# One kernel, two reorderings: mask, weights and tiles loaded and multiplied chunk by chunk, and the small model's first turns split between the halves of the tiles beside them

## The reference

```
w  = w0 * repeat32x32(sum of each 32x32 block of mask > 0)
x1 = norm(x + x @ w.T)
x2 = norm(x1 + x1 @ w1.T + bias1 + adapter of the sequence)
x3 = norm(x2 + small_model(x2))
out = norm(x3 + x3 @ w3.T + bias3 + routed mixture of 8 adapters)
```

## Time and profile before

| | |
|---|---|
| median of 3 runs | 1832.55 us (1831.14 to 1834.01) |
| the profiled execution's own time | 1833.98 us |
| its span | 1832.3 us |
| PE busy | 1723.3 us, 94% of the span |
| DVE, ACT, POOL busy | 1066.5, 654.6, 436.3 us |
| granted PE clock, mean | 0.964 of full |
| share of the chain that ended last | PE 82%; issue, DVE, DMA 4% each |

### The profile page before, as it was taken

One profiled execution on the slowest core, in us unless ns is written; L12 is line 12 of the kernel. 1 busy time (PEld: TensorE's weight loads), 2 busy tenths in 40 slices (PEclk: granted clock), 3 DMA queues, 4 the chain that ended last, 5 costly groups with the idle time before them and its releaser, 6 DMA issues.

```text
span 1832.3 us, 23328 instructions
## 1 busy us (share of the span) xinstructions
PE 1723.3 (94%) x8154; PEld 1382.9 (75%) x8154; DVE 1066.5 (58%) x2049; ACT 654.6 (36%) x967; POOL 436.3 (24%) x380
## 2 busy tenths in 40 slices
PE   5999999999999999998699999997599899899898
PEld 4788888888888888887566666665478678678686
DVE  5433443345555555575577777766467567567553
ACT  2433333333333333222244545544233333333321
POOL 3111111100000000000366777743112112112110
PEclk9999999999999999999789999997699999899999
DMA  6323333333333332322010000004436536536421
GB/s 242 104 92 116 112 118 118 118 125 111 111 103 117 107 111 102 142 75 90 26 44 35 1 1 1 1 25 162 169 118 227 174 119 225 182 111 219 147 101 58
DMA packets 81543, 199.78 MB, mean 109 GB/s; under 512 B 9747, under 2 KB 26131, under 8 KB 81171
## 3 DMA queue, kind: packets, MB, share of 16 engines
q1 hardware_dynamic: 60690, 129.07, 21.5%
q10 hardware_dynamic: 20736, 69.22, 9.4%
HBM read 125.89 MB, written 72.35 MB: 108 GB/s over the span
## 4 chain that ended last, share of the span: by engine, by line
PE 82%; issue 4%; DVE 4%; DMA 4%; ACT 3%; POOL 2%; SPq 1%; ACTq 0%; POOLq 0%; DVEq 0%
PE ps L643 18%; PE ps L645 17%; PE ps L644 17%; PE ps L825 7%; PE ps L657 3%; PE ps L770 3%; PE ps L816 2%; PE ps L817 2%; PE ps L815 2%; DMA a_in<-in_expert_a 2%; PE ps L776 2%; PE ps L731 1%; PE ps L793 1%; PE ps L707 1%; PE ps L709 1%
## 5 line engine op out<-in xcount | busy, mean ns | idle before, releaser
L643 PE MATMUL ps<-wall_x,x_hi 128*128 128x512 f32 x1008 | 401.6, 398 | 10.7 <-DVE wall_x L1276 5.3
L645 PE MATMUL ps<-wall_x,x_lo 128*128 128x512 f32 x1008 | 396.1, 393 | 0.0
L644 PE MATMUL ps<-wall_x,x_hi 128*128 128x512 f32 x1008 | 395.7, 393 | 0.0
L1838 POOL TENSOR_TENSOR rstd<-var_eps,minus_half 128x1 f32<-128x1 f32 x96 | 77.2, 804 | 933.6 <-DVE minus_mean L1311 926.6
L1302 DVE BATCH_NORM_STATS2 stats<-row 128x6 f32<-128x512 f32 x192 | 133.0, 694 | 182.0 <-ACT row L996 177.6
L643 PEld LDWEIGHTS ps<-wall_x,x_hi 128*128 128x128 f32 x1008 | 191.5, 190 | 55.4 <-issue 13.3
L645 PEld LDWEIGHTS ps<-wall_x,x_lo 128*128 128x128 f32 x1008 | 191.2, 190 | 41.2
L644 PEld LDWEIGHTS ps<-wall_x,x_hi 128*128 128x128 f32 x1008 | 191.7, 190 | 38.4
L643 PE MATMUL ps<-wall_y,x_hi 128*128 128x512 f32 x512 | 204.0, 398 | 2.8 <-POOL wall_y L1845 2.8
L645 PE MATMUL ps<-wall_y,x_lo 128*128 128x512 f32 x512 | 200.4, 391 | 0.0
L644 PE MATMUL ps<-wall_y,x_hi 128*128 128x512 f32 x512 | 200.3, 391 | 0.0
(11 more groups left out here) (236 smaller groups left out, 2944.4 us busy)
## 6 DMA issues: line engine op xcount, KB each, us to landing
x_scratch<-row ACTq DMA_DIRECT2D x64, 512.0 KB, 2.8
x_in<-x_scratch SPq DMA_DIRECT2D x64, 512.0 KB, 4.0
w_in<-in_w_t SPq DMA_DIRECT2D x96, 256.0 KB, 3.0
cx<-x_scratch SPq DMA_DIRECT2D x32, 512.0 KB, 4.2
x_scratch<-cx ACTq DMA_DIRECT2D x32, 512.0 KB, 2.7
out<-row ACTq DMA_DIRECT2D x32, 512.0 KB, 2.6
x_in<-in_x_t SPq DMA_DIRECT2D x29, 512.0 KB, 3.4
w_more<-in_w_t SPq DMA_DIRECT2D x32, 256.0 KB, 3.6
```

Of the source, the lines that this page charges most:

```text
L643: pe.matmul(bank, hi[:, k], wall[:, k, 0, cols], start=(k == 0), stop=False)
L644: pe.matmul(bank, hi[:, k], wall[:, k, 1, cols], start=False, stop=False)
L645: return pe.matmul(bank, lo[:, k], wall[:, k, 0, cols], start=False, stop=(k == KC - 1))
L1838: pool.tensor_tensor(rstd[:, i:i + 1], var_eps[:, i:i + 1], minus_half[:, 0:1], ALU.pow)\
```

## The change

At the start, the loads go chunk by chunk with tile k beside chunk k, PE does two tiles of a chunk before the third, and DVE, ACT and PE have a new order. At the end of layer B, the early turns' steps are moved from the end of each tile's work to places between its halves, and the loads of `h` move from j = 4 to j = 5.

```diff
# SP
-            for k in range(2):
+            for k in range(KC):
                 load_w0(k)
-            for t in range(FIRST):
-                sp.dma_start(x_first[:, t], a["x_t"][t]).then_inc(first_loaded[t], 16)
-            for k in range(2, KC):
-                load_w0(k)
+                if k < FIRST:
+                    sp.dma_start(x_first[:, k], a["x_t"][k]).then_inc(first_loaded[k], 16)
...
-                if b + 1 == BATCHES and j == 4:
+                if b + 1 == BATCHES and j == 5:
                     sp.wait_ge(table_done, 1)
                     for n in range(UNITS - 2):
                         load_h(n)
# PE: first_products(k) becomes first_product(k, t), one tile
-            for k in range(3):
-                spread_blocks(k)
-            for k in range(KC):
-                first_products(k)
+            spread_blocks(0)
+            spread_blocks(1)
+            first_product(0, 0)
+            first_product(0, 1)
+            spread_blocks(2)
+            first_product(1, 0)
+            first_product(1, 1)
+            spread_blocks(3)
+            first_product(0, 2)
+            first_product(1, 2)
+            for k in range(2, KC):
+                first_product(k, 0)
+                if k + 2 < KC:
+                    spread_blocks(k + 2)
+                first_product(k, 1)
+                first_product(k, 2)
...
+                if s > B_END - EARLY:
+                    spread_rstd1(s - 1 - B_END + EARLY)
                 product(s, 1)
...
+                if s >= B_END - EARLY:
+                    variance1(s - B_END + EARLY)
                 if i >= 1:
                     turn_y(s - 1)
-                if s >= B_END - EARLY:
-                    turn_of(order, s - B_END + EARLY)
# ACT
-            w0_hi(0)
-            split_x(0)
-            w0_hi(1)
-            split_x(1)
-            split_x(2)
-            for k in range(2, KC):
+            for k in range(KC):
+                if k < FIRST:
+                    split_x(k)
                 w0_hi(k)
...
+                if s > B_END - EARLY:
+                    silu_x(s - 1 - B_END + EARLY)
+                if s >= B_END - EARLY:
+                    square1(s - B_END + EARLY)
                 if i >= 1:
                     split_y(s - 1)
-                if s >= B_END - EARLY:
-                    turn_of(order + order_end, s - B_END + EARLY)
# DVE: the loop over KC + 2 steps is replaced by
+            compare(0)
+            split_x(0)
+            add_identity(0)
+            block_sums(1)
+            w0_low(0)
+            compare(1)
+            split_x(1)
+            block_sums(2)
+            add_identity(1)
+            compare(2)
+            w0_low(1)
+            split_x(2)
+            block_sums(3)
+            add_identity(2)
+            compare(3)
+            for k in range(2, KC):
+                w0_low(k)
+                if k + 2 < KC:
+                    block_sums(k + 2)
                 if k + 1 < KC:
+                    add_identity(k + 1)
+                if k + 2 < KC:
+                    compare(k + 2)
...
                 half_stats(s, 0)
+                if s > B_END - EARLY:
+                    scale1(s - 1 - B_END + EARLY)
...
                 if s >= B_END - EARLY:
-                    turn_of(order + order_end, s - B_END + EARLY)
+                    turn = s - B_END + EARLY
+                    if turn == 2:
+                        scan(0)(0)
+                        scan(1)(0)
+                    if turn >= 1:
+                        rotate(turn - 1)
+                    take_var1(turn)
```

More of the change, by code:

```diff
@@ L624, in spread_blocks, with first_product @@
                   .then_inc(spread, 1)
-            def first_products(k):
+            def first_product(k, t):
                 pe.wait_ge(w0_hi_ready, k + 1)
                 pe.wait_ge(w0_lo_ready, k + 1)
[L629 to L638, removed]
+                if k == 0:
+                    pe.wait_ge(hi_ready, t + 1)
+                    pe.wait_ge(lo_ready, t + 1)
+                for half in range(2):
+                    last = terms(t, half, k, wall_x)
+                    if k == KC - 1:
+                        last.then_inc(mm_done, 1)
             def terms(s, half, k, wall):
@@ L1671, in _ @@
             block_sums(0)
-            for k in range(KC + 2):
-                if k + 1 < KC:
[L1674 to L1682, removed]
+            compare(0)
[17 more added lines that the diff above has]
+                    block_sums(k + 2)
+                if k + 1 < KC:
+                    add_identity(k + 1)
+                if k + 2 < KC:
+                    compare(k + 2)
             split_x(FIRST)
```

## The result

The changed kernel takes 1816.67 us (median of 7 runs, 1814.64 to 1820.36) against 1834.01 (7 runs of the kernel before beside it and earlier, 1824.74 to 1838.32). The ratio is 0.9911, 95% interval 0.9889 to 0.9933, which is 16.3 us gained (12.3 to 20.4); the two medians are 17.3 apart. The forecast was 1817.5, with 1812 to 1825 as range. The profiled execution's span is 1814.9 us (before 1832.3).

A forecast was written before the change was run, and what follows sets the result against it. PE was taken as the bound from 60 to 840 us and as starved at both ends of that stretch. Gains of 3.0 and 12.1 made 15.1, 1833.98 to 1818.9, or 1817.5 against the median 1832.55; range 1812 to 1825.

The forecast's parts named there:

- Sum: Whole kernel: 3.0 us from the start plus 12.1 from layer B's end, 15.1 gained; chance 0.68.
- The start until PE begins: Start: new load and engine order brings PE's first product at 12.4 us instead of 20.70, 8.3 earlier.
- The row's price for the hold: Start: DVE's low part, begun inside a POOL mask, took 1.75 us instead of 1.22, ending 1.07 after it.
- The start until its end: Start through chunk 7: done at 56.15 us instead of 58.98; 3.0 gained taken, bounds 1.5 and 5.1.
- Rival 1: Start gains nothing: DVE late at each chunk, PE stops and half rate lasts longer; 1820.5 us, chance 0.12.
- Nothing in it is tied to absolute time: PE's stretch from 60 to 840 us: moving its work earlier moves the end by as much.
- rival 4: Later stalls meet the clock's steps differently; slower by 0.2% needs 38 us more at half rate; chance 0.02.
- The end of layer B: Layer B's end: 10.7 us until turn_y(6) plus 1.4 behind it, 12.1 gained; bounds 9 to 14.
- The margins: Layer B's end: squares in time for variance1(0) by 0.5 us; rstd1(0) ready at 855.3, needed 856.3, margin 1.0.
- Rival 2: Layer B's end: stalls move, spread_rstd1 waits mid-tile between the halves; 1823 us, chance 0.11.
- rival 3: Turns 3 and 4: pipeline stands at DVE's mixes and PE's projection, part two worth 1; 1828.5 us, chance 0.05.
- the loads: Layer B's end: 4.7 us less from 848.21 to turn_x, plus 1.6 of half rate to 858.

The follow-up runs named there:

- Experiment 6: Changed kernel with POOL's masks of chunks 3 to 7 cut to one column in 32, the rest left unmasked; 1810.77 us in one run.
- experiment 1: Kernel before with only the start's part of the change, end of layer B as before; 0.9993, 1831.57 us.
- experiment 2: Kernel before with only the end of layer B changed (early turns' steps between the halves, loads of h at j = 5); 0.9931, 1820.62 us.
- experiment 4: Changed kernel with the loads of h put back to j = 4; 0.9948 of the kernel before, 1822.36 us.
- experiment 5: Changed kernel with DVE's mask sums behind compare from chunk 2 on and PE spreading three chunks ahead; 0.9894 of the kernel before, 1813.52 us.
- experiment 7: Changed kernel with DVE's mixes moved from the end of turn 3 to where DVE waited for the variance; 0.9902 of the kernel before, 1812.35 us.
- experiment 8: Changed kernel with the one-column bias product in two parts, half a product apart; 0.9926 of the kernel before, 1818.08 us.
- experiment 9: Changed kernel with both the mask sums behind compare and the mixes early; 0.9887 of the kernel before, 1810.91 us.
- experiment 10: On top of experiment 9, take_var1(2) ahead of tile 62's split and tile 63's statistics ahead of turn 2's recurrences; 0.9874 of the kernel before, 1808.80 us.
- experiment 3: Kernel before with one line changed, the loads of h at j = 5 instead of 4; 0.9991, 1832.11 us.
- experiment 11: Changed kernel again, unaltered, beside experiments 9 and 10; 0.9908 of the kernel before, 1814.49 us.

## Why the prediction was right

**Sum.** 15.1 was forecast, 16.3 measured (12.3 to 20.4). It is right for its main term, the end of layer B. That the whole came so close is in part luck: in the profile the kernel was 11.8 us ahead at the row of tile 63, not 15.1, because a half-rate stretch at 795 took 3.4, and gained 5.5 behind that row for which the sum has no term.

**The start until PE begins.** 12.4 forecast, 13.12 measured: the first mask and tile landed 0.2 and 1 us later than I had them, and the rest followed. The row's price for the hold was right in kind (both orders occur in the profile after).

**The start until its end.** 56.15 forecast, 56.15 measured, but by two errors that cancel. The clock rose before 17.5 (the spread at 17.46 takes 0.30), not at about 25, so chunk 2 began at 27.0, after 0.6 of waiting, and not at 28.3. And four periods were held, at 5.2, where I had counted three at 5.1 and one of 4.35. Experiment 6 shows the mechanism itself. Rival 1 (the start gains nothing) is wrong at its place.

**"Nothing in it is tied to absolute time."** This was the step that failed. In the changed kernel's two profiles and in experiments 1, 2 and 4 to 10 a half-rate stretch of 3.4 or 6.8 us follows the bias product near 795; in the kernel before and in experiment 3 it is missing. PE is busy there in all. So 2.8 us gained at 56 were 0.6 lost at 835 in the profile shown. All ten profiles with the new start have it and one of the three with the old one (experiment 2), so it does not need the new order, but that the new order makes it likelier is not excluded; what decides stays open.

**Behind the row of tile 63.** Here the sum has no term, and rival 4, which looked for a change of half rate there, priced only a loss. PE stands idle 72.5 us there before and 73.0 after, but is busy for 862.1 and 856.0, with 118.7 and 99.6 us at half rate: the clock makes the difference. It is not in the turns just behind the row, since the variance 90 us later comes within 0.2 us of the same place. Part of it is scatter, as the other profile of the changed kernel has 926.5 to go and 86.8 at half rate. But it is not one execution alone. Taking the gain by time (ratio) and subtracting the gain at the row of tile 63 in the one profile leaves 4.5 for the changed kernel, 5.0 for it in experiment 11, and 4.1, 4.4, 5.7 and 2.9 in experiments 2, 4, 5 and 8; in 1 and 3, where the steps were not moved, it leaves 1.2 and -2.1. So some 4 us seem to go with the moved steps, though each row is from one execution. By what way is not shown.

**The end of layer B.** 12.1 forecast, 12.4 measured from table to row, in the change and in experiment 2. The margins held: variance1(0) came at once, rstd1(0) was ready at 855.9, half a tile done at 856.9 (margin 1.0). The 6.49 us behind the last product stood as 6 to 7 in the forecast. Rival 2 (a wait between the halves) did not happen, rival 3 (given back in turns 3 and 4) not either: something like it happened to experiment 10. I had the loads at 4.7 + 1.6 = 6.3 as a term that stands by itself; alone they are worth 4.2 locally, and the rest needs the steps too. The term was right only within the whole.

**The Trainium skill.** SBUF — State Buffer, "Who interferes with whom", has the rule of the shared port that the first part rested on, and that a VectorE reduce never contends. This case agrees: a low part of 2.77 behind a mask, a mask of 2.88 behind a split, a mask sum of 1.20 beside a mask.

## What to carry to other kernels

When two engines exclude one another on two-input instructions, order the queue so that the other engine's long instruction falls beside work with one input, here a reduce beside the mask: 2.8 us from chunk 2 on (2.0 by tile 3 of that profile) for moving DVE's mask sum and PE's spread. When a pipeline is fed beside another loop, put each step where its input is already there, and look at the loads on the same queue too: order and load were worth 5.3 and 4.2 us apart and 12.4 together. And a saving far ahead of the end has to be followed to the next half-rate stretch before it is booked.

## What the hardware showed that I had not expected

The clock fell with PE 100% busy by the profile: 3.40 of 3.40 us busy before 794.6, then 0.50 for 6.8 us. The fall came 2.3 to 4.2 us after the start of 16 bias products of one column (32 instructions, 3.6 us at full rate) in 11 of 13 profiles (in that of experiment 8 with half of them ahead of it). They are the only thing there that is not in other tiles, but the one attempt to test it (8) did not separate it.

A multiplication of 128x32 on POOL took 0.29 us in experiment 6 with no two-input instruction beside it, and 1.18 to 1.25 beside a low part of 1.22 on DVE, so a small instruction can be held for a long one as well:

```profile
24.53 0.29 POOL L1861 TENSOR_TENSOR w_in<-w_in,block_on 128x32 f32<-128x32 f32 x1 [2.98 <-DVE block_on L1274]
28.88 1.25 POOL L1861 TENSOR_TENSOR w_in<-w_in,block_on 128x32 f32<-128x32 f32 x1 [4.06 <-DVE block_on L1274]
```
